# Attention of a four-layer graph network on one Trainium2 core: score tiles of 768 and 896 columns replaced by tiles of 1024

## What is computed

```python
n, d = x.shape                       # 3327, 128
h = Wq.shape[0] // d                 # 8
scale = d ** (-0.5)
q = (x @ Wq.T).reshape(d, n, h)      # 128 batches of 3327 x 8
k = (x @ Wk.T).reshape(d, n, h)
v = (x @ Wv.T).reshape(d, n, h)
a = jnp.einsum('dnh,dmh->dnm', q, k) * scale
a = a + adj + adj
a = jax.nn.softmax(a, axis=2)
out = jnp.einsum('dnm,dmh->dnh', a, v)
out = out.reshape(n, h * d) @ Wo.T
```

## Time and profile before

| | |
|---|---|
| median of 3 runs | 11192.38 us (11191.38 to 11200.26) |
| the profiled execution, its own time | 11190.28 us |
| its span, first to last instruction | 11188.5 us |
| attention in it, first to last VectorE instruction of the phase | 712.07 to 10643 us |
| busy share of the span: PE, DVE, ACT, POOL | 92%, 89%, 93%, 73% |
| granted TensorE clock, mean | 0.982 of 2.4 GHz |

### The profile page before, as it was taken

The page is one execution under the profiler, slowest core; times in us unless marked ns, Lnnn a source line. Parts: engine busy times, 40 slices in busy tenths (PEclk is TensorE's granted clock), DMA queues, the critical chain, the costliest instruction groups (busy, mean ns, idle before and its releaser), DMA issues. The chain is left out here.

```text
span 11188.5 us, 369392 instructions
## 1 busy us (share of the span) xinstructions
PE 10310.4 (92%) x138582; PEld 5288.1 (47%) x138582; DVE 9981.1 (89%) x10846; ACT 10396.8 (93%) x8697; POOL 8142.6 (73%) x4112
## 2 busy tenths in 40 slices
PE   6869999999999999999899999999899999999988
PEld 5525555555455555555444444444444444444483
DVE  7469999999899999999899999999899999999958
ACT  3569999999999999999999999999999999999926
POOL 0038888888788888888788888888788888888800
PEclk7989999999999999999999999999999999999999
DMA  9974343443543443444433333333433333333364
GB/s 386 317 213 61 61 63 61 62 63 61 96 63 61 62 63 61 62 62 68 88 54 55 55 53 56 53 56 52 85 55 54 55 53 56 53 56 52 53 205 177
DMA packets 452184, 957.38 MB, mean 86 GB/s; under 512 B 100327, under 2 KB 396398, under 8 KB 401038
## 3 DMA queue, kind: packets, MB, share of 16 engines
q1 hardware_dynamic: 452076, 955.91, 43.0%
HBM read 799.88 MB, written 155.64 MB: 85 GB/s over the span
## 5 line engine op out<-in xcount | busy, mean ns | idle before, releaser
L1157 DVE SCALAR_TENSOR_TENSOR a_probs<-ps,adj_ring 128x768 f32<-128x768 f32 (+1 forms) x9216 | 8977.6, 1020 | 715.4 <-PE ps L1047 568.3
L1131 POOL TENSOR_TENSOR a_pool_probs<-a_pool_probs,adj_ring 128x768 f32<-128x768 f32 (+1 forms) x4096 | 8131.9, 1985 | 1827.7 <-ACT a_pool_probs L1113 1792.9
L1117 ACT ACTIVATE a_probs<-a_probs 128x1536 f32<-128x1536 f32 (+3 forms) x4096 | 8219.2, 2007 | 41.1 <-DVE a_probs L1157 40.8
L1047 PE MATMUL ps<-a_q,a_k 34*128 34x384 f32 (+1 forms) x26624 | 4450.9, 406 | 602.8 <-ACT a_pool_probs L1113 371.5
L1113 ACT ACTIVATE a_pool_probs<-ps 128x768 f32<-128x768 f32 (+1 forms) x4096 | 4501.5, 1099 | 35.3 <-PE ps L1047 35.1
L1067 PE MATMUL ps<-a_probs,a_v 128*9 128x192 f32 (+1 forms) x73728 | 4008.9, 340 | 0.0
L1047 PEld LDWEIGHTS ps<-a_q,a_k 34*128 34x128 f32 x26624 | 2174.7, 184 | 3131.9 <-ACT a_pool_probs L1113 1195.4
L1067 PEld LDWEIGHTS ps<-a_probs,a_v 128*9 128x9 f32 x73728 | 1944.0, 91 | 1276.5 <-issue 121.9
L1067 PE MATMUL ps<-a_pool_probs,a_v 128*9 128x192 f32 (+1 forms) x32768 | 2216.0, 342 | 1.3 <-POOL a_pool_probs L1131 1.3
L1067 PEld LDWEIGHTS ps<-a_pool_probs,a_v 128*9 128x9 f32 x32768 | 486.9, 88 | 986.2 <-issue 983.4
L595 POOL MEMSET v_rows<- 128x512 f32 x2 | 1.9, 1038 | 405.3 <-POOLq L88 405.3
(11 more groups left out here) (171 smaller groups left out, 1908.3 us busy)
## 6 DMA issues: line engine op xcount, KB each, us to landing
a_k<-k_parts SPq DMA_DIRECT2D x2048, 208.0 KB
a_v<-v_ext SPq DMA_DIRECT2D x512, 117.0 KB, 3.4
adj_t<-tr SPq DMA_DIRECT2D x26, 1664.0 KB, 20.3
g0tile<-adj_t SPq DMA_DIRECT2D x26, 1664.0 KB, 10.3
g2tile<-adj_t SPq DMA_DIRECT2D x26, 1664.0 KB
nat<-in_adj SPq DMA_DIRECT2D x25, 1663.5 KB, 18.2
e_nat<-in_adj SPq DMA_DIRECT2D x25, 1663.5 KB, 6.9
a_q<-q_parts SPq DMA_DIRECT2D x2048, 12.0 KB
```

The lines of the kernel that those rows point to most:

```text
L1047: ins = nc.tensor.matmul(ps[:, place + bank:place + bank + half], k_tile[b][row:row + SCORE_ROWS, P * j:P * (j + 1)].bitcast(F32R), q_tile ...
L1117: nc.scalar.activation(sums_of(k, nb), sums_of(k, nb), ACT.Exp, scale=2.0).then_inc(sums_exped, 1)
L1131: nc.gpsimd.tensor_tensor(probs(k, nb), probs(k, nb), ring.block(c, j, nb * P), ALU.mult).then_inc(multiplied, 1)
L1157: v.scalar_tensor_tensor(out=halves(probs(k, nb)), in0=score(j, nb), scalar=SCALE / 2, in1=halves(ring.block(c, j, nb * P)), op0=ALU.mult, ...
```

## The change

The query blocks are cut otherwise: chunk 0 has only two of them (256 columns), and chunks 1, 2 and 3 have eight (1024 columns). A unit of chunk 0 takes four batches side by side, 4 x 256 columns, so that each tile is 1024 columns wide throughout. That makes 32 + 3 x 128 = 416 units.

- In a unit of chunk 0 each of the four batches has its own keys. Two key tiles more lie in the ring (`ring.keys`), and a block's scores are four matmuls of 256 columns with four weight loads. The weighing matmuls were four already; each now takes its batch's values (`v_tile` has four). VectorE and GpSimd read one 256-column block of adjacency for all four batches (`adj_of`). SyncE issues 28 DMAs of keys and queries for a unit of chunk 0.
- The ring has 28 slots of 1024 columns, two more than a chunk's blocks. Of chunk 1, parts 0 and 1 are loaded at the start, parts 2 and 3 when chunk 0 is done (its keys and its adjacency lie there). Of chunks 2 and 3 all four parts wait for the last unit of the chunk before: part 0 for the use of blocks 0 to 3.
- ScalarE has one loop for all units. A reserve for DMAs that GpSimd issues is made smaller; all DMAs here are issued by SyncE.

```diff
-CHUNKS = ((14, 6), (20, 6), (0, 7), (7, 7))
-GROUPS_OF_CHUNKS = ((6, 2), (7, 2))
-WIDEST = 7
+CHUNKS = ((24, 2), (0, 8), (8, 8), (16, 8))
+ACROSS = 8
+WIDTH = ACROSS * P
+SHARE = WIDTH // 4
...
-ADJ_SLOTS = BLOCKS + 6
+ADJ_SLOTS = BLOCKS + 2
+FEW_AT, KEYS_AT = 21, (13, 17)
...
-            for part in ring.EARLY:
+            for part in range(len(ADJ_PARTS)):
                 ring.load(sp, 0, part, True)
...
+def many(c):
+
+    return ACROSS // CHUNKS[c][1]
...
+    def block(self, c, j):
+        width = CHUNKS[c][1] * P
+        at = WIDTH * ((BLOCKS * (c - 1) + j) % ADJ_SLOTS) if c else WIDTH * FEW_AT + width * j
+        return self.tile[:, at:at + width]
...
+        def adj_of(c, j):
+            block = ring.block(c, j)
+            return block.unsqueeze(1).to_broadcast([P, 4, SHARE]) if many(c) > 1 else block
...
+            for b in range(2):
+                load(0, b, b)
+                load_v(0, v_of_unit(0, b), b)
...
+            for part in range(2):
+                next_part(0, part)
...
+                if more:
+                    all_scored(done - 1)
+                    load(c + 1, 0, 0)
+                    if c:
+                        for part in range(len(ADJ_PARTS)):
+                            sp.wait_ge(ring.loaded[part], ring.ready(c, part, n_pool > 0))
+                        used(c, ADJ_PARTS[0][1] - spare)
+                        next_part(c, 0)
+                    sp.wait_ge(batch_summed, done - 1)
+                    load_v(c + 1, v_of_unit(c + 1, 0), 0)
+                sp.wait_ge(stored[1], (done // 2 - 1) * per_store)
+                store(c, done, last - 1, 0)
+                if more:
+                    if c:
+                        for part in (1, 2):
+                            used(c, ADJ_PARTS[part][1] - spare)
+                            next_part(c, part)
+                    all_scored(done)
+                    load(c + 1, 1, 1)
+                    if c:
+                        used(c, ADJ_PARTS[3][1] - spare)
+                    else:
+                        next_part(c, 2)
+                        used(c, BLOCKS)
+                    next_part(c, 3)
...
+                half = SHARE if several else WIDTH // 2
+                for n in range(1 + several):
+                    for row, bank in halves_of_rows:
+                        at = place + bank + half * n
+                        ins = nc.tensor.matmul(ps[:, at:at + half],
+                                               keys[b][n][row:row + SCORE_ROWS, P * j:P * (j + 1)].bitcast(F32R),
+                                               q_tile[b][row:row + SCORE_ROWS, half * n:half * (n + 1)].bitcast(F32R),
+                                               start=True, stop=True)
```

More of the change, by code:

```diff
@@ L789, in _ @@
                 nc.gpsimd.memset(k_tile[b][:, :], 1.0)
+                nc.gpsimd.memset(ring.keys[b], 1.0)
             pool.wait_ge(mosts, 2)
@@ L860, in attention_phase @@
     name = f"a{len(pool_blocks)}_"
-    turns = BATCHES // 2
     units = 2 * BLOCKS
@@ L969, in store @@
                 sp.wait_ge(acc_read, ready)
                 for g in range(4):
-                    at = first * P + 32 * nb * g
-                    sp.dma_start(o_of[d, :, at:at + 32 * nb], o_tile[b][32 * g:32 * g + VG, 0:32 * nb]).then_inc(stored[b], LOAD)
-            load(0, 0, 0)
-            load_v(BATCHES - 1, 0)
-            for part in range(len(ADJ_PARTS)):
-                if not n_pool and part in ring.EARLY:
-                    sp.wait_ge(ring.loaded[part], ring.ready(0, part, True))
-                if not n_pool or part not in ring.EARLY:
-                    ring.load(sp, 0, part, n_pool > 0)
@@ L981, in _, with next_part @@
-            load(0, 1, 1)
-            load_v(BATCHES - 2, 1)
+                    batch, at = (d, CHUNKS[c][0] * P + SHARE * g) if many(c) == 1 else (4 * d + g, CHUNKS[c][0] * P)
+                    sp.dma_start(o_of[batch, :, at:at + SHARE], o_tile[b][32 * g:32 * g + VG, :]).then_inc(stored[b], LOAD)
+            def next_part(c, part):
+                ring.load(sp, c + 1, part, n_pool > 0)
+            for b in range(2):
+                load(0, b, b)
+                load_v(0, v_of_unit(0, b), b)
@@ L983, in _ @@
+            for part in range(len(ADJ_PARTS)):
+                sp.wait_ge(ring.loaded[part], ring.ready(0, part, True))
+                if not n_pool:
+                    ring.load(sp, 0, part, False)
+                    sp.wait_ge(ring.loaded[part], ring.ready(0, part, False))
+            for part in range(2):
+                next_part(0, part)
             spare = ADJ_SLOTS - BLOCKS
             for c in range(len(CHUNKS)):
-                done = c * BATCHES
+                begin, done = units_before[c], units_before[c + 1]
+                last = done - begin - 1
@@ L1024, in _, with scores @@
                 sp.wait_ge(stored[0], done // 2 * per_store)
-                store(c, done + 1, BATCHES - 1, 1)
+                store(c, done + 1, last, 1)
             for b in range(2):
-                sp.wait_ge(stored[b], len(CHUNKS) * turns * per_store)
+                sp.wait_ge(stored[b], units_before[-1] // 2 * per_store)
         @block.tensor
         def _(pe):
-            def scores(k, nb, batch, pair, begun):
+            def scores(k, several, unit, pair, begun):
                 of, j = divmod(k, BLOCKS)
@@ L1043, in scores @@
                 elif begun or of or dve_rank[j] >= DVE_SLOTS:
[L1044 removed]
+                    pe.wait_ge(added, (unit + of) * n_dve + (dve_rank[j] + 1 - DVE_SLOTS))
                 place = score_place(j)
[L1046 to L1050 removed]
+                half = SHARE if several else WIDTH // 2
@@ L1051, in scores, with weigh @@
                 ins.then_inc(scores_ready[by_pool[j]], 1)
-            def weigh(k, nb, batch, pair):
+            def weigh(k, several, unit, pair):
                 of, j = divmod(k, BLOCKS)
@@ L1122, in _ @@
             if n_pool:
-                for c, (_, nb) in enumerate(CHUNKS):
-                    with pool.Fori(c * turns, (c + 1) * turns) as pair:
+                for c in range(len(CHUNKS)):
+                    with pool.Fori(units_before[c] // 2, units_before[c + 1] // 2) as pair:
                         for k in range(units):
@@ L1145, in _ @@
             dve.wait_ge(cleared, 1)
-            for c, (_, nb) in enumerate(CHUNKS):
-                with dve.Fori(c * turns, (c + 1) * turns) as pair:
+            for c in range(len(CHUNKS)):
+                with dve.Fori(units_before[c] // 2, units_before[c + 1] // 2) as pair:
                     for k in range(units):
                         b, j = divmod(k, BLOCKS)
-                        batch = pair * 2 + b
+                        unit = pair * 2 + b
                         if b == 0 and j in (begin for begin, _ in ADJ_PARTS):
```

216 lines of the change are left out of this document (103 added, 113 removed).

## The result

The changed kernel takes 11103.58 us (median of 4 runs, 11102.6 to 11109.5), the kernel before 11196.32 us beside it (11191.38 to 11205.9). The ratio is 0.9917, 95% interval 0.9900 to 0.9934: 0.8% faster, 93 us between the medians, where 87 had been worked out from the profiled execution of before. The profiled execution has a span of 11100.5 us where that of before has 11188.5.

The account below looks back on a forecast made before the run. ScalarE was taken to pace every steady unit, with idle time at chunk changes. Steady units -118, four-batch units +2, changes +21, start +7 and end +1 gave -87 us against 11190.3: 11103 us, range 11075 to 11152.

Parts of the forecast that it names:

- The gain a unit: Steady units: 416 of 23.42 us replace 512, saving 96 times the fixed 1.232 us, -118 us.
- Four-batch units: Chunk 0's 32 units: +2 us for TensorE's narrower matmul pairs, 0 for GpSimd's adjacency reads with 12 as bound.
- Rival B: Four-batch units: TensorE paces them at 24.7 us a unit, +39 us, 11142 us in all; chance 0.15.
- Chunk changes: Three chunk changes: larger ring reloads stall ScalarE 18, 28 and 28 us, 74 for 53 before, +21 us.
- Rival C: Chunk changes: reloads run at 305 GB/s, stalls 47 us in all, giving 11076 us; chance 0.15.
- rival E: Chunk changes: reloads fall to 110 GB/s, stalls of 94, 94 and 51 us, giving 11268 us; chance 0.04.
- Start: Start of attention: +6.8 us for 28 DMAs, -5.3 for a ring wait gone, +6 for late keys; sum +7 us.
- the ring wait: First unit: its 5.25 us wait goes, chunk 0's adjacency being small and early, -5.3 us.
- the keys: Start: unit 2's keys, queued behind ring blocks, land about 772 where TensorE wants them about 766, +6 us.
- The end: End of the kernel: only the last unit's wider leftovers were priced, +1 us.
- The sum: Whole kernel: -118 + 2 + 21 + 7 + 1 = -87 us against the profiled 11190.3 us, giving 11103 us.
- Rival D: All units: ScalarE's fixed part isn't fixed, 0.2 us more a unit takes the whole gain, 11190 us; chance 0.06.

Follow-up runs that it names:

- the splits: Changed kernel with two more ScalarE exponentials a unit: one set of three split into two instructions, 11288.5 us, or two sets of two split, 11174.4 us.
- experiment 7: Changed kernel with the four score matmuls of each block issued twice in the four-batch units: 11197.0 us, ratio 1.0005 to the kernel before.
- experiment 3: Changed kernel with the exponential over each set of three sums blocks split into 1024 and 2048 columns: 11288.5 us, ratio 1.0090 to the kernel before.
- experiment 6: Changed kernel with the eighteen sums blocks in six sets of three, ring of three, for eight sets and ring of four: 11598.0 us, ratio 1.0364.
- experiments 9 and 10: Changed kernel with the new chunk's second-unit keys loaded behind the ring's reload, run in two lots: 11087.0 us (ratio 0.9909) and 11083.7 us (0.9905).
- experiment 4: Changed kernel with sets of three split, and score matmuls of blocks 2 and 15 issued twice in one-batch units: 11181.6 us, ratio 0.9993.
- experiment 5: Changed kernel with the exponentials of two sets of two split, the sets of three left whole: 11174.4 us, ratio 0.9986 to the kernel before.
- experiments 1 and 2: Ring reloads left out, later chunks reading earlier blocks again: in the changed kernel 11038.3 us (ratio 0.9869), in the kernel before 11134.2 us (0.9955).

## Why the prediction was right

**The gain a unit** held to the third digit: 23.425 us measured for 23.42, in the one-batch and the four-batch units alike: 405 of the 416 gaps between copies are 23.39 to 23.45 us, and the other eleven are at the start, the changes and the end. In the changed kernel's second trace it is 23.413. 416 units give 9745 us in place of 9860.6, -116 us for -118: the unit is 6 ns longer than worked out. The kernels without reloads confirm it apart from the changes: 113 us for units, start and end together, where -118 + 2 + 7 + 1 = -108 had been worked out, and the terms measured in the profiled pair (the sum below, without the changes) give -107. Their runs can't tell 5 us. What was not quite as the prediction had it is what the remainder of 1.232 us consists of. It divides into 0.05 us for an instruction that reads PSUM and 0.10 to 0.12 for one that reads SBUF, not into 16 equal parts. Here that did no harm, since the change removes whole units and both kinds in proportion.

The rule of the Trainium skill (ScalarE: Activation LUTs, What ACT_TABLE_LOAD costs), by which each instruction costs 93 ns and the gain would be 143 us, is right for the instructions that the splits add (90 ns each) and too high for the mean of this kernel's (77 ns).

**Four-batch units**: 0 us for the +2 taken. The broadcast operand costs GpSimd nothing (2396 ns in either kind of unit, extended gave 2400), and VectorE neither (1221 ns in either). TensorE's pair of 256 columns is 0.12 us, the lower end of the bounds. Rival B is out by more than the sum could tell: it had TensorE at 24.7 us a unit, and experiment 7 puts it at 20.5. Busy time and named waits understate TensorE's room, which here follows ScalarE's pace. How its busy time comes to hold this room is not shown. The upper end of the forecast's range added 12 us for GpSimd to B (11154 us rather than the 11152 given); of two engines at 23.8 and 24.7 us a unit only the slower would have paced, so the two don't add. No run came near it.

**Chunk changes**: +19.5 us (72.7 - 53.2) for +21. Singly 16.8, 28.8 and 27.1 for 18, 28 and 28, and the blocks landed after 57.5 us for 58. At the second and third change there are three waits of VectorE, at blocks 6, 13 and 19, where two were named; the sum is the same, since what counts is when the last part lands. What the mechanism lacks is TensorE's clock. It took all of ScalarE's idle time for waiting until block 19, but 2.6 to 2.9 us of it came after that block in the kernel before, and 3.5, 5.1 and 3.0 us after the change, at a granted clock that had fallen to 0.50. The prediction carried the old amount along unseen, in the time at which block 19 was due. So of the +19.5 us some 3.4 (11.6 - 8.2) come behind the last block, and that the singly forecast stalls fit within 1.2 us is in part luck. Rival C, reloads at 305 GB/s, and rival E, at 110, are both out.

**Start**: VectorE begins 11.2 us later for 6.8, the worst sized term. Two things are in it. The preparation ahead of attention ended 3.1 us later, and nothing shows this to be an effect of the change: VectorE's last two instructions of it, which write `s_part`, begin at 686.1 us before and 689.2 after, and anywhere from 678.0 to 692.0 in the eleven later traces. From there to VectorE's first instruction of attention it is 26.0 us before and 34.0 after, so the change costs 8.0 in this pair. The later traces have 27.3 with narrow units and 33.2 to 34.6 with wide ones, so it costs between 5.9 and 8.6, and the 6.8 for the issue of 28 DMAs in place of 14 lies inside. The other part of the term, -5.3 for the ring wait and +6 for the keys, came out as -2.2: the keys of unit 2 cost the 5.40 us, but ScalarE's idle time in the first units outside its first wait is 10.4 us before and 8.2 after.

**The end**: 545.5 us from the last copy to the end of the span before (10642.98 to 11188.5), 544.3 after (10556.25 to 11100.5), where nothing had been forecast. The last wait for TensorE ahead of that copy grew from 4.58 to 5.22 us, the last unit's leftovers for which +1 stood.

**The sum**: -116 + 0 + 19.5 + 11.2 - 2.2 + 1 - 1.3 is -88 for the profiled pair, whose spans differ by 88.0. The forecast's -87 has a gain 2 us too large and a start 2 us too small in it, 2 us for the four-batch units that did not come, changes 1.5 us too dear, and an end 1.3 us shorter that it didn't have. Each of these has been seen by itself, and no large error hides another. But that small ones cancel to 1 us is luck, and so is that the median came out at 11103.6 for 11103: 3 us of the start are the preparation's drift, and the four runs span 7 us.

**Rival D**, a fixed part that isn't fixed, is out at 23.425. But experiment 3 shows a way in which it could have come true that the prediction hadn't thought of: not on ScalarE, but through TensorE's clock. TensorE in the changed kernel waits 0.75 us twice a unit. With 0.85 us there, as in the split kernel, the unit costs 0.29 us more (23.89 - 23.605), 0.29 x 416 = 120 us, and the whole gain would have been gone.

## What to carry to other kernels

When one engine paces a steady loop, two sizes of the unit give its fixed and its streaming part, and the difference of two copies over a hundred units gives them to a few nanoseconds; a third size can then be forecast. Check as well what kind of instruction the fixed part belongs to before pricing one added or removed singly. Look at the waits of TensorE, even where it is not the bound: a wait that grows by a tenth of a microsecond can cost more than the edit that made it grow. Keep what alternates through a single buffer alternating (experiment 6), and have the order of a DMA queue put the last part wanted ahead of what has a unit's time left (experiments 9 and 10, 8 and 15 us). After a stall, look at TensorE's granted clock before putting all of the idle time down to what was waited for.

## What the runs showed of the hardware that was not expected

- The granted clock fell to 0.50 for some 3.5 us at a time, in a kernel whose TensorE is busy for 93% of the stretch, once its two waits a unit had gone from 0.75 us to between 0.82 and 0.85 (experiment 3). Apart from the start, the chunk changes and the end it fell only in the units with the long wait: 0.98 in those and 1.00 in the others of one and the same kernel (experiment 4). At a clock of 1.00 TensorE was busy for 870.01 us of 937 (experiment 5) and even for only 856.79 (experiment 6), with no wait over 0.77 us.
- Around the waits for ring blocks at a chunk change the granted clock stands at 0.50 for 3 to 24 us at a time, before the change and after it, and ScalarE idles for 2.6 to 5.1 us more behind the last block. Where no block is late it stays at 1.00 (experiments 1 and 2).
- ScalarE's fixed part beside its columns is 0.05 us for an exponential out of PSUM and 0.10 to 0.12 us for one out of SBUF in its own place, start to start (the means of 0.907, 1.802 and 2.677 us in the changed kernel).
- Score matmuls of 256 columns with their weight loads go through at 0.12 us a pair in two row groups (experiment 7).
